# Two attention stages split apart, with a new hand-written order on every engine

## What is computed

```
x = x + tanh(g_xattn[0]) * attn0(layernorm(x), ctx)          # first attention
x = x + tanh(g_ffn[0])   * experts(layernorm(x))             # 8 experts, 2 for each row
x = x + tanh(g_xattn[1]) * attn1(layernorm(x), ctx, ctx)     # second attention
x = x + tanh(g_ffn[1])   * ternary_ffn(layernorm(x))

attn0: q = x @ Wq; k, v = split(context @ Wkv)               # 16 heads of 16
       q, k = rope(q), rope(k)
       return softmax(q k^T / 4) v @ Wo + bo
attn1: qn = layernorm(q)*g + b                               # a second norm of the rows
       kk = (layernorm(k)*g + b) @ Wk.T; vv = (layernorm(v)*g + b) @ Wv.T
       y = softmax((qn @ Wq.T) kk^T / 4) vv
       return (y * sigmoid(qn @ Wg.T + bg)) @ Wo.T
```

## Time and profile before

| | us |
|---|---|
| median of three runs | 3129.7 (3127.54 to 3130.5) |
| the run that was profiled | 3133.01 |
| span of the profiled execution | 3131.2 |
| first attention, 0 to 677.9 | 677.9 |
| experts, 677.9 to 1418.17 | 740.3 |
| second attention, 1418.17 to 2438.0 | 1019.8 |
| feed-forward, 2438.0 to 3131.2 | 693.2 |

### The profile page before, as it was taken

How to read it: one execution, slowest core, us unless ns; L and a number is a source line. 1 busy time by engine, 2 the same in 40 slices (tenths; PEclk the granted TensorE clock), 3 DMA queues, 4 the chain that set the end, 5 groups by cost and what they waited for, 6 DMA issues and landing times. The chain is left out here.

```text
span 3131.2 us, 51627 instructions
## 1 busy us (share of the span) xinstructions
PE 2117.5 (68%) x14617; PEld 1602.1 (51%) x14617; DVE 1671.4 (53%) x3810; ACT 1387.5 (44%) x2665; POOL 1211.5 (39%) x1320
## 2 busy tenths in 40 slices
PE   5777777754318999993887777777777344444443
PEld 3666666644317999982555555555555222222222
DVE  4666666745422332322343433334343699889887
ACT  3555555532103444432443443434343366666665
POOL 2222222215662222226433434343330356555554
PEclk8999999975558999995777877778788566666666
DMA  2111111134332222324222222232310100000000
GB/s 63 48 47 45 46 46 46 38 121 166 115 116 82 89 87 85 89 80 92 63 48 62 52 56 62 46 65 43 65 37 24 52 21 27 27 27 27 27 20 20
DMA packets 177273, 185.64 MB, mean 59 GB/s; under 512 B 23746, under 2 KB 170947, under 8 KB 176131
## 3 DMA queue, kind: packets, MB, share of 16 engines
q1 hardware_dynamic: 152578, 149.49, 16.1%
q0 software_dynamic: 24576, 34.62, 5.3%
HBM read 109.82 MB, written 74.24 MB: 59 GB/s over the span
## 5 line engine op out<-in xcount | busy, mean ns | idle before, releaser
L536 DVE TENSOR_REDUCE a_mneg<-a_ps_m 128x4 f32<-128x480 f32 x512 | 311.7, 650 | 230.1 <-PE a_ps_m L730 229.9
L413 ACT ACTIVATE a_probs<-a_ps_e 120x512 f32<-120x512 f32 x512 | 290.6, 597 | 192.9 <-PE a_ps_e L743 192.7
L628 DVE TENSOR_SCALAR a_k<-a_ps_t,a_pairmask 96x960 bf16<-96x960 bf16 x64 | 45.7, 714 | 435.4 <-ACT a_k L456 429.8
L1156 POOL TENSOR_TENSOR e_h_lo<-e_h 128x256 bf16<-128x256 f32 (+1 forms) x213 | 130.6, 613 | 326.2 <-DVE e_h L1365 326.2
L1365 DVE TENSOR_TENSOR e_h<-e_s,e_ps_ab 128x256 f32<-128x256 f32 (+1 forms) x213 | 89.4, 420 | 293.8 <-ACT e_s L1191 293.8
L1384 PE MATMUL e_ps_ab<-e_xt_hi,e_w_hi 128*128 128x256 bf16 (+1 forms) x852 | 233.1, 274 | 0.1
L1384 PE MATMUL e_ps_ab<-e_xt_hi,e_w_lo 128*128 128x256 bf16 (+1 forms) x852 | 232.9, 273 | 0.0
L1384 PE MATMUL e_ps_ab<-e_xt_lo,e_w_hi 128*128 128x256 bf16 (+1 forms) x852 | 232.8, 273 | 0.0
L357 POOL DMA_INDIRECT a_xa<-back_rows,a_where x128 | 204.9, 1601 | 31.4 <-issue 30.4
L1613 POOL TENSOR_TENSOR f_y<-f_tap 128x512 f32<-128x512 f32 x128 | 163.4, 1277 | 108.6 <-ACT f_tap L1636 108.6
L321 POOL TENSOR_TENSOR a_ve<-a_mv,a_oneeps 128x3 f32<-128x3 f32 x32 | 6.2, 195 | 491.1 <-DVE a_mv L581 490.8
(11 more groups left out here) (242 smaller groups left out, 5589.2 us busy)
## 6 DMA issues: line engine op xcount, KB each, us to landing
e_xe<-sent_rows SPq DMA_DIRECT2D x71, 272.0 KB, 2.9
back_rows<-e_yo SPq DMA_DIRECT2D x71, 256.0 KB, 2.2
x_rows<-a_x SPq DMA_DIRECT2D x64, 256.0 KB, 3.2
a_xa<-in_x SPq DMA_DIRECT2D x32, 256.0 KB, 3.6
a_xr<-in_x SPq DMA_DIRECT2D x32, 256.0 KB, 2.9
e_xa<-x_rows SPq DMA_DIRECT2D x8, 1024.0 KB
a_xa<-x_rows SPq DMA_DIRECT2D x32, 256.0 KB
x_rows<-a_xa SPq DMA_DIRECT2D x32, 256.0 KB, 3.1
```

What stands on the lines that cost most here:

```text
L413: nc.scalar.activation(probs[0:S, 2 * i:2 * i + 2, :].rearrange("p h n -> p (h n)"), ps_e[0:S, i % 2, :], ACT.Exp, scale=SCALE).then_inc(b ...
L536: nc.vector.tensor_reduce(mneg[:, i // 4, 4 * (i % 4):4 * (i % 4) + 4], ps_m[:, i % 2, 0:4 * S].rearrange("p (h s) -> p h s", s=S), AX_X, ...
```

## The change

`attention` becomes two functions, `attention_first` and `attention_second`. Both have six stages, run by a new `stepped`, in which an engine's step is one flat list: each piece takes the batch `b = at(k)` that is k steps behind. Heads no longer go in number order, and pieces of different stages alternate more finely. Signals are regrouped by stage; PSUM tiles are `ps_a` to `ps_d`, and the helper `freed` waits for the last reader of a tile. Experts and feed-forward are as before.

In the first attention:

- SP loads the rows a second time, turned, from a new input `xT` (256 KB a batch) straight into `xt`. GpSimd no longer writes `xn`, PE no longer turns rows, ACT no longer copies them.
- The mean goes into the weights once, at the start: PE multiplies Wq with a matrix of 1/256 and DVE subtracts it. The factor 1/sqrt goes into the split of the queries: ACT L368 in two instructions with a scale for each row, DVE L449 in two.
- The sums `qf` and `kf` move from DVE to POOL.
- The second half of `k2` moves from DVE to ACT, the first half of `q2` from ACT to DVE (L412).
- ACT copies the result of V in two halves, one after each half of the product.

In the second attention:

- The gate is computed turned: weights stationary, rows moving, into `ps_b`. Its bias comes in ACT's tanh, now two instructions (L996); the bias products are gone.
- DVE multiplies gate and turned result straight from PSUM into `ot`; `og` and ACT's copy (L419) are gone. PE turns the result ahead of the gate and not behind it.
- Norming rows moves from POOL to DVE (L1114). The copy of V and one half of the copy of the result move from ACT to DVE; of `k2`, ACT and DVE keep a half each.
- SP's list is laid out anew; the load of `xa` for the batch in stage 0 stands behind the load of `xr` and ahead of the store of the result and of the merged rows.

The core of the diff:

```diff
+def landed(eng, sems, batch):
+    if batch is not None:
+        eng.wait_ge(sems[batch.par], 16 * (batch.half + 1))
+def stepped(eng, step, stages, fixed):
+    def at(n):
+        return lambda s: Batch(n - s, (n - s) // 2, (n - s) % 2) if 0 <= n - s < B else None
+    def within(batch):
+        return lambda s: batch.back(s) if s else batch
+    for n in range(fixed):
+        step(at(n))
+    with eng.Fori(0, (B - fixed) // 2) as k:
+        step(within(Batch(2 * k + fixed, k + fixed // 2, 0)))
+        step(within(Batch(2 * k + fixed + 1, k + fixed // 2, 1)))
+    for n in range(B, B + stages - 1):
+        step(at(n))
...
+                b = at(0)
+                if b is not None:
+                    pe0.wait(sp, at(2), "q")
+                    nc.sync.dma_start(xt[:, b.par, :, :], a["xT"][b.n]).then_inc(t_ld[b.par], 16)
+                    dve0.wait(sp, at(2), "bn")
+                    nc.sync.dma_start(xa[:, b.par, :, :], x_t[b.n]).then_inc(x_ld[b.par], 16)
+                    pe1.wait(sp, at(2), "kv")
+                    nc.sync.dma_start(ca[:, b.par, :, :], a["ctxT"][b.n]).then_inc(c_ld[b.par], 16)
+                b = at(4)
+                if b is not None:
+                    nc.sync.dma_start(xr[:, b.par, :, :], x_t[b.n]).then_inc(r_ld[b.par], 16)
+                b = at(5)
+                if b is not None:
+                    dve5.wait(sp, b, "fin")
+                    nc.sync.dma_start(out_t[b.n], x1[:, b.par, :, :]).then_inc(o_st[b.par], 16)
...
-                    last = nc.gpsimd.tensor_scalar(xn[:, t, :], xa[:, p, t, :], mv[:, t, 0:1], rstd[:, t:t + 1],
-                                                   ALU.subtract, ALU.mult)
...
+                b = at(0)
+                if b is not None:
+                    gp0.wait(gp, at(1), "rstd")
+                    dve0.wait(gp, b, "var")
+                    nc.gpsimd.tensor_tensor(ve[:, :], mv[:, :, 1], eps[:, :], ALU.add).then_inc(gp0.sem, 1)
+                b = at(5)
+                if b is not None:
+                    dve5.wait(gp, at(6), "fin")
+                    landed(gp, r_ld, b)
+                    nc.gpsimd.tensor_tensor(xb[:, :, :], xr[:, b.par, :, :], bias[:, :].unsqueeze(1).to_broadcast([P, NT, D]), ALU.add).then_inc(gp5.sem, 1)
+                b = at(0)
+                if b is not None:
+                    gp0.wait(gp, b, "ve")
+                    nc.gpsimd.tensor_tensor(rstd[:, b.par, :], ve[:, :], half[:, :], ALU.pow).then_inc(gp0.sem, 1)
+                    dve0.wait(gp, b, "rope_q")
+                    nc.gpsimd.tensor_tensor(qf[:, :, :], rc[:, :, :], rs[:, :, :], ALU.add).then_inc(gp0.sem, 1)
+                b = at(1)
+                if b is not None:
+                    dve1.wait(gp, b, "rope_k")
+                    nc.gpsimd.tensor_tensor(kf[0:S, :], k_cos[0:S, :], k_sin[0:S, :], ALU.add).then_inc(gp1.sem, 1)
...
+                b = at(0)
+                if b is not None:
+                    pe1.wait(act, at(1), "qTa")
+                    gp0.wait(act, b, "qf")
+                    for t in range(NT):
+                        last = nc.scalar.activation(qx[:, t, :, 0:32], qf[:, t, :].rearrange("p (c d) -> p c d", d=32),
+                                                    ACT.Copy, scale=rstd[:, b.par, t:t + 1])
+                    last.then_inc(act0.sem, 1)
...
-                    nc.vector.tensor_tensor(qf[:, :, :], rc[:, :, :], rs[:, :, :], ALU.add).then_inc(fv.sem, 1)
-                    nc.vector.tensor_tensor(qx[:, :, :, 64:96], q_src,
-                                            qx[:, :, :, 0:32], ALU.subtract).then_inc(fv.sem, 1)
...
+            dve.wait_ge(s_fold, 1)
+            for c in range(KC):
+                nc.vector.tensor_tensor(wq[:, c, :], wq[:, c, :], ps_a[:, 0:D], ALU.subtract).then_inc(s_fold, 1)
...
+                    nc.vector.tensor_copy(qx[:, :, :, 32:64], qx[:, :, :, 0:32])
+                    for t in range(NT):
+                        last = nc.vector.scalar_tensor_tensor(qx[:, t, :, 64:96], qf[:, t, :].rearrange("p (c d) -> p c d", d=32), rstd[:, b.par, t:t + 1],
+                                                              qx[:, t, :, 0:32], ALU.mult, ALU.subtract)
+                    last.then_inc(dve1.sem, 1)
...
+            product(ps_a[:, 0:D], [(level[:, :], wq[:, c, :]) for c in range(KC)]).then_inc(s_fold, 1)
+            pe.wait_ge(s_fold, 1 + KC)
...
+            def step(at):
+                b = at(0)
+                if b is not None:
+                    nc.sync.dma_start(where[:, b.par, :], places[b.n]).then_inc(w_ld[b.par], 16)
+                b = at(4)
+                if b is not None:
+                    landed(sp, m_st, b)
+                    nc.sync.dma_start(xr[:, b.par, :, :], res_t[b.n]).then_inc(r_ld[b.par], 16)
+                b = at(0)
+                if b is not None:
+                    dve1.wait(sp, at(2), "norm")
+                    landed(sp, m_st, at(2))
+                    nc.sync.dma_start(xa[:, b.par, :, :], x_t[b.n]).then_inc(x_ld[b.par], 16)
+                b = at(1)
+                if b is not None:
+                    gp1.wait(sp, at(3), "cnorm")
+                    nc.sync.dma_start(ca[0:S, b.par, :], a["ctx"][b.n]).then_inc(c_ld[b.par], 16)
+                b = at(5)
+                if b is not None:
+                    dve5.wait(sp, b, "fin")
+                    nc.sync.dma_start(out_t[b.n], x1[:, b.par, :, :]).then_inc(o_st[b.par], 16)
+                b = at(1)
+                if b is not None:
+                    landed(sp, y_ld[1][0], b)
+                    landed(sp, y_ld[1][1], b)
+                    nc.sync.dma_start(res_t[b.n], xa[:, b.par, :, :]).then_inc(m_st[b.par], 16)
...
+                    for e in range(KC):
+                        last = nc.scalar.activation(gate[:, b.par, e, :], ps_b[:, e * N:(e + 1) * N], ACT.Tanh, bias=half_bg[:, e:e + 1], scale=0.5)
+                    last.then_inc(act3.sem, 1)
...
+                b = at(1)
+                if b is not None:
+                    gp1.wait(dve, b, "rstd")
+                    for t in range(NT):
+                        last = nc.vector.tensor_scalar(xn[:, t, :], xa[:, b.par, t, :], mv[:, t, 0:1], rstd[:, b.par, t:t + 1],
+                                                       ALU.subtract, ALU.mult)
...
-                        last = product(ps_x[:, i * D:(i + 1) * D], terms(xt[:, mid.par, :, :], slice(i * P, (i + 1) * P), wq, D) + bias_terms)
-                    last.then_inc(de.sem, 1)
...
+                    freed(pe, (act2, at(2), "q2b"), (act3, at(4), "tanh"))
+                    for e in range(KC):
+                        last = product(ps_b[:, e * N:(e + 1) * N], [(wq[:, c, D + e * P:D + (e + 1) * P], xt[:, b.par, c, :]) for c in range(KC)])
+                    last.then_inc(pe3.sem, 1)
...
```

1626 lines of the change are left out of this document (1037 added, 589 removed).

## The result

The changed kernel takes 2506.0 us (2505.5 to 2508.0), the kernel before 3129.1; the ratio is 0.801, 95% interval 0.7996 to 0.8024. The profiled execution has a span of 2504.3.

The account below looks back on a forecast made before the run. The prediction took short waits between PE, DVE and ACT to bound both attentions; 1433.5 us unchanged plus 539 (steps of 15.5) and 611.5 (steps of 17.5) gave a span of 2584, forecast 2585, range 2510 to 2720.

Parts of the forecast that it names:

- A step is bound by a loop of short waits: Both attentions before: steps of 20.0 and 30.5 us, bound by waits between PE, DVE and ACT, not by work.
- TensorE's work at full clock, 13.9 and 16.3 us: PE's summed work per step after the change, first and second attention: 13.9 and 16.3 us.
- Length of a step: 15.5 and 17.5: Forecast step after, first and second attention, in us; hand walk gave 14.3 to 14.7 and 16.2 to 16.5 before additions.
- The lower bound, 14.2: First attention: shortest step the forecast allowed, 14.2 us, with 17.5 as the upper bound.
- First ends at 80 and 92, draining 52 and 60: First and second attention: us until the first batch ends, and us of draining after 26 full steps.
- Experts and feed-forward stay: The two parts whose code stays: 740.3 and 693.2 us, 1433.5 in all, unchanged.
- Half clock costs a wait twice: Second attention before: PE's 3.01 us wait for L607 costs itself and the work behind it at half clock.
- My slower rival: Both attentions: PE pauses some 3 us a step, all its work at half clock; span about 3390; chance 0.02.
- VectorE's work 12.8 and 13.8: VectorE's summed work per step after the change, first and second attention: 12.8 and 13.8 us.
- rival 1: First attention: GpSimd's whole 4.4 us falls on DVE, which bounds the step at 17.2; about 2627 us; chance 0.07.
- The ring of transfers: Second attention: load, gathers, norm, stores and landings bound the step at about 21.5 us; about 2690; chance 0.17.
- Orders block each other: Both attentions: hand-written lists make waits anew, steps of 18.55 and about 25 us; about 2858; chance 0.12.

Follow-up runs that it names:

- sum_earlier_in_before: Kernel before, VectorE's sum that reads the projection (L607) moved ahead of the split of the keys in both attentions: 2965.6 us; first attention 727.0, second 799.7.
- gate_waits: Changed kernel, second attention's gate products behind the projection, waiting for VectorE's read; in the first, GpSimd's `xb` moved behind `qf`: first 489.4 us, second 644.4.
- long_pause: Changed kernel, second attention's gate behind the projection and seven more 0.75 us sums on VectorE ahead of the one it waits for: second attention 857.6 us against 577.4.
- score_earlier: Changed kernel, one maximum score of the first attention (L613) moved on TensorE ahead of the keys-and-values product and two scores: first attention 520.7 us against 492.0.

## Why the prediction was wrong by 3%, step by step

- *A step is bound by a loop of short waits, which the new order removes.* Right: PE's idle fifth of a step is gone in both parts. For the second attention `sum_earlier_in_before` shows with one move that order brings half of the gain, and `gate_waits` shows it backwards. For the first no run separates the new order from the work moved and left out; only the sums on GpSimd (25 us) and the place of one score (29) of its 186 us were measured.
- *TensorE's work at full clock, 13.9 and 16.3 us.* Right: steps of 14.0 and 16.4 with PE busy throughout.
- *Length of a step: 15.5 and 17.5.* This step failed. To a walk of 14.3 to 14.7 I added the lock between VectorE and GpSimd beside `xb`, to 16.2 to 16.5 a wait of about 1 us for a gather, because VectorE's list is so full. The steps are 14.0 and 16.4. The lock came, 1.0 us of VectorE's time a step, but was worth 3 us in the whole part, since VectorE's 13.2 us with it still fit beside TensorE's 13.9; the wait for a gather didn't come (VectorE's norm of the gathered rows waits 0.8 us in 350). 1.5 x 26 = 39 us and 1.1 x 26 = 29 of the 79 lie here. The walk of the lists was better evidence than the caution put on it.
- *The lower bound, 14.2.* It stood above TensorE's own sum of 13.9, so the range left out the plainest case, that PE never waits. With 13.9 and 16.0 it would have reached down to about 2503.
- *First ends at 80 and 92, draining 52 and 60.* 75.2, 86.7, 49.5 and 61.5: 10 us of the miss are the fill of both parts, 1 their draining.
- *Experts and feed-forward stay.* 738.8 and 696.1; code that is the same, off by 1.5 and 2.9, or by 1.7 and 2.1 with the boundaries read alike.
- *Half clock costs a wait twice.* Right for the kernel before, where 3.01 us of idle PE stood among other pauses of 0.5 to 1.6 in a step of 30: 2.6 us of idle and 4.0 of slower work went together. As a rule it was wrong: 2.90 us beside one pause of 0.90 left the gate's products at full speed in 13 of 19 steps, 5.53 us in none of six. My slower rival, all work at half clock from pauses of some 3 us a step, has no support in these runs: even `long_pause` had 0.88 over its steady stretch.
- *VectorE's work 12.8 and 13.8.* 246.92 / 260 x 13.9 = 13.2, and 13.4. The lock came in the first (1.0 us a step), not GpSimd's whole 4.4: rival 1's mechanism, at a quarter of its size and with nearly nothing on the time. (Its 17.2 is 1.7 and not 1.6 above 15.5, 2 us more.) The Trainium skill, "SBUF — State Buffer", section "Who interferes with whom", says that an instruction of VectorE with two inputs in SBUF and one of GpSimd that reads SBUF block each other. L449 at 1500 ns beside `xb` and 480 apart from it agree with it, and so does `xb` at 1503 against 1265. L589 of the kernel before doesn't: it took its usual 0.42 to 0.46 us in 24 of the 28 steps in which it ran beside `xn`.
- *The ring of transfers.* Close to the step's length and not the bound.
- *Orders block each other.* No, but `score_earlier` and `gate_waits` show how near that is: a piece in a wrong place costs 29 to 67 us at once.

What stays open is which part of the rest of the second attention's gain, some 220 us beyond the one move, belongs to which of the moved pieces; only the norm's place (40) and the gate's (67) were measured. In the first attention most of the gain is open in the same way.

## What to carry to other kernels

In a software pipeline whose engines are all under 80% busy, look first for one instruction that stands late in its engine's list and that another engine waits for: moving that one call gave 220 us here in one stage, and cost 49 in another where something else was waited for behind it. When an order is laid out anew and the hand walk says that the fullest engine never waits, take that engine's own sum as the forecast and as the lower end of the range, and add waits only to the upper end. Where two lists are full, look at both: in the first attention here 28 us of work taken from one and 32 from the other gave 2 and 3 us, both together 11. Where one piece has to come in time, what counts is the work ahead of it and its slack (0.5 us a step for L1140 here), and not its engine's busy share.

## What the runs showed of the hardware

- The granted clock stayed at 1.00 with two pauses of PE of 0.9 us a step. With one of 2.9 and one of 0.9 it fell in 6 of 19 steps, with one of 5.53 and one of 0.9 in each step looked at, to 0.50 for some 6 us, and came back with PE busy.
- One DVE operation with two inputs in SBUF (128x256) took 1500 ns beside a GpSimd sum of two tiles and 480 apart from it, and the GpSimd sum took 1503 ns in place of 1265: both sides pay.
- The second attention with the same code took 577.4 to 581.3 us in four profiled runs, the first 490.9 to 493.5 in five.
